# Three differences of two operands become one difference and four clamped tensor_scalar instructions in an RWKV and mixture-of-experts kernel

## The chip, the cores and the metric

The kernel runs on one core of a Trainium2 chip. Its time is the device time of one execution in microseconds (us), the median of three runs. A profile of one further execution gives every engine's instructions with their start and length. The engines are TensorE (PE, with its weight loads as PEld), VectorE (DVE), ScalarE (ACT), GpSimd (POOL) and SyncE (SP, which only issues DMAs here).

## What is computed

Sixteen sequences of 512 tokens and 256 channels go through two blocks, each with a layer norm ahead of it and a residual sum behind it. The first is an RWKV attention. Cut to what matters here:

```
w = -exp(time_decay)                 # per channel
step(aa, bb, pp; kk, vv):            # over the 512 tokens
    ww  = time_first + kk
    p   = max(pp, ww)
    y   = (exp(pp-p)*aa + exp(ww-p)*vv) / (exp(pp-p)*bb + exp(ww-p))
    p2  = max(pp + w, kk)
    e1  = exp(pp + w - p2);  e2 = exp(kk - p2)
    aa, bb, pp = e1*aa + e2*vv, e1*bb + e2, p2
out = (sigmoid(r) * y) @ Wo.T
```

The second block is a causal convolution and pointwise product, a router that picks two of eight experts for each token, the eight experts' products, a root-mean-square norm and a small feed-forward.

## The kernel before

The channels lie on the 128 partitions in two halves (H = 2), the tokens along the free axis, so a tile such as `fd` is 128 x 2 x 512 in f32. Every engine runs a program of its own, in an order written out by hand, and engines meet only at semaphores. One pass of `body(g, f, b, a, n)` works on five sequences at once, each in a later stage: n is normalised and turned, a goes through the recurrence, b through the output projection, f through router and experts, g through the norm and the feed-forward. `schedule` runs the body 20 times, for g = -4 to 15, of which g = 1 to 10 are a loop. A sequence is in stage a in 16 of these bodies: three while the pipeline fills (no g yet), and thirteen, g = 0 to 12, in which both a and g are there. The fill bodies g = -3 and g = -2 have an order of their own (the branch `if on(n) and not on(f)`).

The recurrence is made of scans along the tokens. `running_maximum` scans `pp` (L1128), one scan per half. `differences` writes `fd` = pp(t-1) - pp(t) (L1136) and `gd` = kk - pp(t) (L1137); `difference_sd`, which stands further back in the body, writes `sd` = kk - pp(t-1) (L1140). `decay` holds w. ACT turns `fd` into e1 with w as the bias of the exponential (L778), `gd` into e2 (L780), and `sd` into a sigmoid (L793). Each of the three differences raises the semaphore `diffs` by one. `wkv_step` 0 to 9 are the rest of the recurrence on DVE.

What matters of the order around this, in a body with a and g:

- DVE: scans of `pp`, `differences`, `mix` of xr (L1081), `scale_h(0)` (L1119, writes `hh`), `convolve` (L1073, four instructions), `scale_h(1)` (L1119 again), `difference_sd`, `quotient` (L1109), then `xh`, `wkv_step` 0 and 1, the sum `x1` (L1193), `x1l`, statistics, the copy of the router's logits `lg` (L1228), the picking of experts up to `gap` (L1261), and the weighted sums of the experts (L1295). `scale_h(1)` waits for `rms` from POOL (L413).
- PE: products of xk, xv and xr (L450), the turning of `hh` (L444), the pointwise product, `wdown` (L624), `wo` (L536), the router (L643 to L647), then sixteen groups of experts (L465 to L469) with other work between them.
- ACT: copies of `kk` and `vv`, the exponentials, squares for the norm (L749), tanh, copies of `ht`, the sigmoid, silu, `x1h` (L896), gelu, and then the sixteen silus of the experts (L729); the third of them stands behind `th` (L920), which needs `gap`.

The semaphore `diffs` is also read by the copy of `kk` and by `running_maximum` of the next sequence, which may overwrite `kk` and `pp` only when all differences are done.

Of the kernel before, what the change touches and what calls it, by code (L numbers as in the profile page):

```python
# [18 lines left out]
ALU = mybir.AluOpType  # L19
ACT = mybir.ActivationFunctionType  # L20
# [27 lines left out]
def build(nc, x, vecs, w_attn, w_pw, w_router, w_expert, w_out, w_down, w_up, b_rows, b_down, norm_w, out):  # L48
    B, T, C = x.shape
    H = C // P  # L50
# [9 lines left out]
    with ExitStack() as ctx:  # L60
        def sb(name, shape, dt=F32):
            return ctx.enter_context(nc.sbuf_tensor(name, shape, dt))
# [4 lines left out]
        def sig(name, per):  # L67
            return Signal(ctx.enter_context(nc.semaphore(name)), per)
# [3 lines left out]
        decay = sb("decay", [P, H])  # L72
# [17 lines left out]
        bias = sb("bias", [BP, NROW // BP])  # L90
# [30 lines left out]
        kk = sb("kk", [P, H, T])  # L121
        vv = sb("vv", [P, H, T])
        pp = sb("pp", [P, H, 1 + T])
        fd = sb("fd", [P, H, T])
        gd = sb("gd", [P, H, T])
        sd = sb("sd", [P, H, T])
# [80 lines left out]
        v_ready = sig("v_ready", 2)  # L207
        tr_ready = sig("tr_ready", 2)
        p_ready = sig("p_ready", 2)
        diffs = sig("diffs", 3)  # L210
        e1_ready = sig("e1_ready", 2)
        e2_ready = sig("e2_ready", 1)
        sg_ready = sig("sg_ready", 2)
# [54 lines left out]
        def on(seq):  # L268

            return not isinstance(seq, int) or 0 <= seq < B  # L270
# [413 lines left out]
        def _(act):  # L684
# [4 lines left out]
            def body(g, f, b, a, n):  # L689
# [83 lines left out]
                        act.copy(vv[:, h, :], pk[:, h, :]).then_inc(v_ready.sem, 1)  # L773

                def exponentials():
                    act.wait_ge(diffs.sem, diffs.at(a, 1))
                    for h in range(H):
                        act.activation(fd[:, h, :], fd[:, h, :], ACT.Exp, bias=decay[:, h:h + 1]).then_inc(e1_ready.sem, 1)  # L778
                    act.wait_ge(diffs.sem, diffs.at(a, 2))
                    act.activation(gd[:], gd[:], ACT.Exp).then_inc(e2_ready.sem, 1)  # L780

                def tanh_r():
# [5 lines left out]
                        act.activation(tr[:, h, :], pk[:, h, :], ACT.Tanh, scale=0.5).then_inc(tr_ready.sem, 1)  # L788

                def sigma():  # L790
                    act.wait_ge(diffs.sem, diffs.at(a, 3))
                    for h in range(H):
                        act.activation(sd[:, h, :], sd[:, h, :], ACT.Sigmoid, bias=neg_first[:, h:h + 1],  # L793
                                       scale=-1.0).then_inc(sg_ready.sem, 1)
# [69 lines left out]
                if on(a):  # L864
                    exponentials()
# [17 lines left out]
                if on(a):  # L883
                    sigma()
# [80 lines left out]
        def _(dve):  # L965
            v = nc.vector
# [41 lines left out]
            def body(g, f, b, a, n):  # L1008
# [39 lines left out]
                def residual(i):  # L1048

                    dve.wait_ge(xres_in.sem, xres_in.at(b))  # L1050
                    if on(f):
                        dve.wait_ge(xn2_ready.sem, xn2_ready.at(f))
                        dve.wait_ge(x2t_ready.sem, x2t_ready.at(f))
                    dve.wait_ge(wo_done.sem, wo_done.at(b, i + 1))
                    t = slice(2 * i, 2 * i + 2)
                    v.tensor_tensor(x2[:, t, :], po[:, i], xres[:, t, :], ALU.add).then_inc(x2_ready.sem, 1)

                def stats_proj():

                    dve.wait_ge(x2_ready.sem, x2_ready.at(b))  # L1060
                    if on(f):
                        dve.wait_ge(rstd2_ready.sem, rstd2_ready.at(f))
                    for t in range(NT):
                        v.bn_stats(st2[:, t, :], x2[:, t, :]).then_inc(stats2.sem, 1)

                def convolve(seq):

                    for tap in (1, 2):
                        for h in range(H):
                            dve.wait_ge(tap_ready.sem, tap_ready.at(seq, h + 1))  # L1070
                            if tap == 2:
                                dve.wait_ge(conv.sem, conv.at(seq, h + 1))
                            v.scalar_tensor_tensor(out=cv[:, h, :], in0=xt2[:, h, 2 - tap:2 - tap + T],  # L1073
                                                   scalar=vec[:, 7 - tap, h:h + 1], in1=cv[:, h, :],
                                                   op0=ALU.mult, op1=ALU.add).then_inc(conv.sem, 1)

                def mix(seq, m, dst):

                    for h in range(H):
                        dve.wait_ge(faded[m].sem, faded[m].at(seq, h + 1))  # L1080
                        v.scalar_tensor_tensor(out=dst[:, h, :], in0=xt1[:, h, 1:1 + T], scalar=vec[:, 2 + m, h:h + 1],  # L1081
                                               in1=dst[:, h, :], op0=ALU.mult, op1=ALU.add).then_inc(mixed.sem, 1)
# [12 lines left out]
                def stats_front():  # L1095

                    dve.wait_ge(x_in.sem, x_in.at(n))
                    if on(a):
                        dve.wait_ge(rstd1_ready.sem, rstd1_ready.at(a))
                    for t in range(NT):  # L1100
                        v.bn_stats(st1[:, t, :], xa[:, t, :]).then_inc(stats1.sem, 1)  # L1101

                def quotient():

                    dve.wait_ge(rec_ready.sem, rec_ready.at(b))
                    dve.wait_ge(wkv.sem, wkv.at(b))
                    if on(f):
                        dve.wait_ge(wo_done.sem, wo_done.at(f))
                    v.tensor_tensor(rwkv[:], num[:], den[:], ALU.mult).then_inc(rwkv_ready.sem, 1)  # L1109

                def scale_h(i):

                    dve.wait_ge(rms_ready.sem, rms_ready.at(g, 3 * i + 3))

                    if on(g - 1):
                        dve.wait_ge(t4_done.sem, t4_done.at(g - 1))
                        dve.wait_ge(xh_ready.sem, xh_ready.at(g - 1))
                    for t in range(2 * i, 2 * i + 2):
                        v.scalar_tensor_tensor(out=hh[:, t, :], in0=po[:, i, t % 2, :], scalar=rms[:, t:t + 1],  # L1119
                                               in1=normw[:], op0=ALU.mult, op1=ALU.mult).then_inc(h_ready.sem, 1)  # L1120

                def running_maximum():

                    if on(b):
                        dve.wait_ge(diffs.sem, diffs.at(b))
                    for h in range(H):
                        dve.wait_ge(k_ready.sem, k_ready.at(a, h + 1))
                        v.tensor_tensor_scan(pp[:, h, 1:1 + T], decay[:, h:h + 1].to_broadcast([P, T]), kk[:, h, :],  # L1128
                                             NEG_INF, ALU.add, ALU.max).then_inc(p_ready.sem, 1)

                def differences():
                    dve.wait_ge(p_ready.sem, p_ready.at(a))

                    if on(b):
                        dve.wait_ge(wkv.sem, wkv.at(b))
                    v.tensor_tensor(fd[:], pp[:, :, 0:T], pp[:, :, 1:1 + T], ALU.subtract).then_inc(diffs.sem, 1)  # L1136
                    v.tensor_tensor(gd[:], kk[:], pp[:, :, 1:1 + T], ALU.subtract).then_inc(diffs.sem, 1)  # L1137

                def difference_sd():
                    v.tensor_tensor(sd[:], kk[:], pp[:, :, 0:T], ALU.subtract).then_inc(diffs.sem, 1)  # L1140

                if on(n) and not on(f):

                    if on(b):
                        quotient()
                    if on(a):
                        mix(a, 2, xr)
                    stats_front()
                    if on(a):
                        running_maximum()  # L1150
                        differences()
                        difference_sd()
                    if on(b):
                        residual(0)
                        residual(1)
                        stats_proj()
                    if on(a):
                        for i in range(10):
                            wkv_step(i)
                    mix(n, 0, xk)  # L1160
                    if on(b):
                        convolve(b)
                    mix(n, 1, xv)
                    return

                if on(a):
                    running_maximum()
                    differences()
                    mix(a, 2, xr)
# [3 lines left out]
                    convolve(f)  # L1173
                if on(g):
                    scale_h(1)
                if on(a):
                    difference_sd()
                if on(b):
                    quotient()
                if on(g):  # L1180
# [129 lines left out]
                else:  # L1310
                    last_sum()

            schedule(dve, body, {-4: constants, -3: lambda: expert_high_part(0), -2: lambda: expert_high_part(1)})


# [34 lines left out]
```

## Time and profile before

| | |
|---|---|
| median of three runs | 982.94 us (982.54 to 983.36) |
| the profiled execution | 982.2 us |
| its span, first to last instruction | 980.4 us |
| mean granted TensorE clock | 0.965 |
| PE busy | 886.0 us, 90% |
| DVE busy | 863.2 us, 88% |
| ACT busy | 720.5 us, 73% |
| POOL busy | 227.5 us, 23% |

The 1.8 us between the profiled execution's time and its span lie outside the instructions. Busy shares are means over the span; in the thirteen full bodies, one every 55.5 us, PE and DVE are both busy nearly without a break.

### The profile page before, as it was taken

To read this page: it belongs to the slowest core of one execution; us is meant where nothing else is said; L and a number is where in the kernel's file an instruction comes from. 1 tells how busy PE (TensorE), PEld (TensorE's weight loads), DVE (VectorE), ACT (ScalarE), POOL (GpSimd) and SP (SyncE) were. 2 spreads that over 40 slices of the span, in tenths; PEclk is the share of its full clock that TensorE was granted. 3 is DMA by queue.
4 is the path that set the end of the run, shared out by engine and by line. 5 is a ranking of instruction groups with operands and counts; after the bars stand their busy time and mean duration, and the time that the engine had idled before them with its cause. 6 is when DMAs were issued, how large, how long until landed. Compare 5 with 4: busy or idle time off the path is not lost. (4 is left out here: it accounts for less than half of the span.)

```text
span 980.4 us, 15792 instructions
## 1 busy us (share of the span) xinstructions
PE 886.0 (90%) x4288; PEld 483.6 (49%) x4288; DVE 863.2 (88%) x1577; ACT 720.5 (73%) x1233; POOL 227.5 (23%) x477
## 2 busy tenths in 40 slices
PE   3554999999999999999999999999999999969895
PEld 2232455554555555554555555555555555535543
DVE  4999799999999999999999999999999998957562
ACT  4755688786978788787878788687878788545643
POOL 3485222113130222113130222113131221111000
PEclk9776999999999999999999999999999999979998
DMA  6110010101010010101010010101001000100000
GB/s 210 44 43 1 1 44 1 65 1 66 0 43 21 0 64 0 64 0 64 0 42 22 0 64 0 64 0 64 0 22 42 22 22 1 44 1 22 1 22 21
DMA packets 28772, 29.66 MB, mean 30 GB/s; under 512 B 2090, under 2 KB 28484, under 8 KB 28484
## 3 DMA queue, kind: packets, MB, share of 16 engines
q1 hardware_dynamic: 28740, 29.27, 8.8%
q8 instruction: 15, 0.25, 0.1%
q14 instruction: 17, 0.14, 0.0%
HBM read 20.87 MB, written 8.39 MB: 30 GB/s over the span
## 5 line engine op out<-in xcount | busy, mean ns | idle before, releaser
L1295 DVE SCALAR_TENSOR_TENSOR comb<-ye,rw,comb 128x256 f32<-128x256 f32 x448 | 216.3, 483 | 24.9 <-ACT ye L729 10.5
L729 ACT ACTIVATE ye<-pe 128x512 f32<-128x512 f32 x256 | 151.6, 597 | 105.2 <-PE pe L469 90.9
L469 PE MATMUL pe<-weh,x1l 128*128 128x512 f16 x512 | 194.0, 379 | 0.0
L468 PE MATMUL pe<-wel,x1h 128*128 128x512 f16 x512 | 194.0, 379 | 0.0
L467 PE MATMUL pe<-weh,x1h 128*128 128x512 f16 x512 | 194.0, 379 | 0.0
L409 POOL TENSOR_TENSOR msv<-ms,rms_eps_c 128x2 f32<-128x2 f32 x32 | 14.9, 466 | 398.0 <-ACT sq L749 398.0
L465 PE MATMUL pe<-brow,ones 128*128 128x512 f16 x256 | 97.3, 380 | 9.0 <-ACT ye L729 9.0
L380 POOL TENSOR_TENSOR mo<-st 128x4 f32<-128x4 f32 x32 | 12.1, 377 | 317.4 <-DVE st L1101 179.6
L468 PEld LDWEIGHTS pe<-wel,x1h 128*128 128x128 f16 x512 | 50.0, 98 | 60.5
L469 PEld LDWEIGHTS pe<-weh,x1l 128*128 128x128 f16 x512 | 50.1, 98 | 60.4
L467 PEld LDWEIGHTS pe<-weh,x1h 128*128 128x128 f16 x512 | 50.1, 98 | 50.3
L450 PE MATMUL pk<-xk,wa 128*128 128x512 f32 x128 | 64.4, 650 | 11.4 <-issue 8.5
L510 PE MATMUL po<-wout,combt 128*128 128x256 f32 x256 | 69.6, 394 | 0.0
L450 PE MATMUL pk<-xr,wa 128*128 128x512 f32 x128 | 60.3, 615 | 8.4 <-DVE xr L1081 8.4
L444 PE MATMUL pt<-ident,xn 128*128 128x128 f32 x256 | 37.4, 294 | 32.0 <-ACT xn L713 22.3
L450 PE MATMUL pk<-cv,wpw 128*128 128x512 f32 x128 | 59.9, 609 | 4.1 <-DVE cv L1073 4.1
L450 PE MATMUL pk<-xv,wa 128*128 128x512 f32 x128 | 58.7, 602 | 0.0
L536 PE MATMUL po<-wo,rwkv 128*128 128x256 f32 x256 | 58.4, 381 | 0.0
L536 PEld LDWEIGHTS po<-wo,rwkv 128*128 128x128 f32 x256 | 49.2, 192 | 14.1 <-issue 8.2
L444 PEld LDWEIGHTS pt<-ident,xn 128*128 128x128 f32 x256 | 31.3, 151 | 42.0 <-issue 26.4
L450 PEld LDWEIGHTS pk<-xk,wa 128*128 128x128 f32 x128 | 26.5, 210 | 41.5 <-issue 39.8
L1119 DVE SCALAR_TENSOR_TENSOR hh<-po,rms,normw 128x256 f32<-128x256 f32 x64 | 27.9, 478 | 21.3 <-POOL rms L413 21.3
(154 smaller groups left out, 1986.1 us busy)
## 6 DMA issues: line engine op xcount, KB each, us to landing
xa<-in_x SPq DMA_DIRECT2D x16, 512.0 KB, 3.6
xres<-in_x SPq DMA_DIRECT2D x16, 512.0 KB, 4.4
out_y<-yo SPq DMA_DIRECT2D x16, 512.0 KB, 2.9
ye<-in_w_expert SPq DMA_DIRECT2D x2, 1024.0 KB, 6.8
wa<-in_w_attn SPq DMA_DIRECT2D x1, 1024.0 KB, 7.8
wpw<-in_w_pw SPq DMA_DIRECT2D x1, 256.0 KB, 6.0
wout<-in_w_out SPq DMA_DIRECT2D x1, 256.0 KB, 6.2
wdown<-in_w_down SPq DMA_DIRECT2D x2, 64.0 KB, 4.7
```

The costliest lines, as they stand in the source:

```text
L409: nc.gpsimd.tensor_tensor(msv[:, t], ms[:, t], rms_eps_c[:, t], ALU.add).then_inc(rms_ready.sem, 1)
L444: mm = nc.tensor.transpose(pt[:, h, t * P:(t + 1) * P], src[:, t, h * P:(h + 1) * P], ident[:])
L450: mm = nc.tensor.matmul(dst, weight[:, h, m * P:(m + 1) * P], src[:, h, :], start=h == 0, stop=h == H - 1)
L465: nc.tensor.matmul(dst, ones2[:], brow[:, cols], start=True, stop=False)
L467: nc.tensor.matmul(dst, x1h[:, h, tok], weh[:, h, cols], start=False, stop=False)
L468: nc.tensor.matmul(dst, x1h[:, h, tok], wel[:, h, cols], start=False, stop=False)
L469: mm = nc.tensor.matmul(dst, x1l[:, h, tok], weh[:, h, cols], start=False, stop=h == H - 1)
L510: mm = nc.tensor.matmul(dst, combt[:, h, tok], wout[:, h, :], start=False, stop=h == H - 1)
L536: mm = nc.tensor.matmul(po[:, i, t % 2, :], rwkv[:, h, t * P:(t + 1) * P], wo2[:, h, :], start=h == 0, stop=h == H - 1)
L729: act.activation(ye[:, i % NY, :], pe[:, i % 2, :], ACT.Silu, scale=1.0 / WSCALE).then_inc(ye_ready.sem, 1)
L1119: v.scalar_tensor_tensor(out=hh[:, t, :], in0=po[:, i, t % 2, :], scalar=rms[:, t:t + 1], in1=normw[:], op0=ALU.mult, op1=ALU.mult).then_i ...
L1295: v.scalar_tensor_tensor(out=comb[:, t, :], in0=src, scalar=rw[:, t, e:e + 1], in1=comb[:, t, :], op0=ALU.mult, op1=ALU.add).then_inc(comb ...
```

## The change

`sd` is now the first difference, in place of `fd`. `fd` and `gd` are computed from it: pp(t) is the larger of pp(t-1) + w and kk, so that sd - w = kk - (pp(t-1) + w) is positive where kk is the larger. `fd` = max(sd - w, 0), of which ACT takes exp with a scale of -1 and without a bias, and `gd` = min(sd - w, 0). Each is a `tensor_scalar` with w as a per-partition scalar, one instruction per half, since w differs between the halves. DVE waits for `sd` on `diffs` before the first of them. `diffs` now rises by five a sequence. The exponentials wait for each half of `fd` apart, and the sigmoid waits for all five where it waited for all three. `difference_sd` is gone from its place behind `scale_h(1)`.

```diff
-        diffs = sig("diffs", 3)
+        diffs = sig("diffs", 5)
...
                 def exponentials():
-                    act.wait_ge(diffs.sem, diffs.at(a, 1))
-                    for h in range(H):
-                        act.activation(fd[:, h, :], fd[:, h, :], ACT.Exp, bias=decay[:, h:h + 1]).then_inc(e1_ready.sem, 1)
-                    act.wait_ge(diffs.sem, diffs.at(a, 2))
+                    for h in range(H):
+                        act.wait_ge(diffs.sem, diffs.at(a, 2 + h))
+                        act.activation(fd[:, h, :], fd[:, h, :], ACT.Exp, scale=-1.0).then_inc(e1_ready.sem, 1)
+                    act.wait_ge(diffs.sem, diffs.at(a, 5))
...
                 def sigma():
-                    act.wait_ge(diffs.sem, diffs.at(a, 3))
+                    act.wait_ge(diffs.sem, diffs.at(a))
...
-                    v.tensor_tensor(fd[:], pp[:, :, 0:T], pp[:, :, 1:1 + T], ALU.subtract).then_inc(diffs.sem, 1)
-                    v.tensor_tensor(gd[:], kk[:], pp[:, :, 1:1 + T], ALU.subtract).then_inc(diffs.sem, 1)
-
-                def difference_sd():
                     v.tensor_tensor(sd[:], kk[:], pp[:, :, 0:T], ALU.subtract).then_inc(diffs.sem, 1)
+                    dve.wait_ge(diffs.sem, diffs.at(a, 1))
+                    for h in range(H):
+                        v.tensor_scalar(fd[:, h, :], sd[:, h, :], decay[:, h:h + 1], 0.0, ALU.subtract,
+                                        ALU.max).then_inc(diffs.sem, 1)
+                    for h in range(H):
+                        v.tensor_scalar(gd[:, h, :], sd[:, h, :], decay[:, h:h + 1], 0.0, ALU.subtract,
+                                        ALU.min).then_inc(diffs.sem, 1)
...
                 if on(a):
-                    difference_sd()
-                if on(a):
                     quotient()
```

On DVE, in the bodies with a and g, the change reads so (rows with - as before, with + as now, a line number being that of its own kernel):

```order
 L1128 SCALAR_TENSOR_TENSOR pp<-decay,kk 128x512 x2
-L1136 TENSOR_TENSOR fd<-pp 128x1024
-L1137 TENSOR_TENSOR gd<-kk,pp 128x1024
+L1136 TENSOR_TENSOR sd<-kk,pp 128x1024
+L1139 TENSOR_SCALAR fd<-sd,decay 128x512 x2
+L1142 TENSOR_SCALAR gd<-sd,decay 128x512 x2
 L1081 SCALAR_TENSOR_TENSOR xr<-xt,vec,xr 128x512 x2
 L1119 SCALAR_TENSOR_TENSOR hh<-po,rms,normw 128x256 x2
 L1073 SCALAR_TENSOR_TENSOR cv<-xt,vec,cv 128x512 x4
 L1119 SCALAR_TENSOR_TENSOR hh<-po,rms,normw 128x256 x2
-L1140 TENSOR_TENSOR sd<-kk,pp 128x1024
 L1109 TENSOR_TENSOR rwkv<-num,den 128x1024
```

Ahead of xr and the two `hh` stood two instructions of 1024 elements; now one of 1024 and four of 512 stand there, and behind the second `hh` one of 1024 is gone.

On ACT, in the loop, the place of the exponentials (ISA and REGISTER_ALU rows are the sequencer's work for a wait in the loop):

```order
 L737 COPY combt<-pt 128x2x128
-L776 ISA
-L778 ACTIVATE fd<-fd,decay 128x512 x2
+L777 ISA
+L778 ACTIVATE fd<-fd 128x512
+L777 REGISTER_ALU
+L778 ACTIVATE fd<-fd 128x512
 L779 REGISTER_ALU
 L780 ACTIVATE gd<-gd 128x1024
```

The same three instructions stand there as before; the first two lose an operand and each gets a wait of its own.

## Rows read from the trace of the kernel before

**Rows 1.** The page, busy time and share of the span of each engine.

```profile
PE 886.0 (90%) x4288; PEld 483.6 (49%) x4288; DVE 863.2 (88%) x1577; ACT 720.5 (73%) x1233; POOL 227.5 (23%) x477
```

**Rows 2.** PE over time: start, length, instruction, count, idle time before it.

```profile
155.22 1.09 PE L444 MATMUL pt<-ident,hh 128*128 128x128 f32 x8 [0.76 <-DVE hh L1119]
...
372.34 3.63 PE L450 MATMUL pk<-xr,wa 128*128 128x512 f32 x8
376.79 1.09 PE L444 MATMUL pt<-ident,hh 128*128 128x128 f32 x8 [0.81 <-DVE hh L1119]
...
386.32 0.17 PE L643 MATMUL pk<-brow,ones 128*128 128x8 f16 x1
...
390.45 0.39 PE L465 MATMUL pe<-brow,ones 128*128 128x512 f16 x1 [0.24 <-ACT ye L729]
...
394.90 0.39 PE L465 MATMUL pe<-brow,ones 128*128 128x512 f16 x1 [0.36 <-ACT ye L729]
...
820.14 1.09 PE L444 MATMUL pt<-ident,hh 128*128 128x128 f32 x8 [0.81 <-DVE hh L1119]
```

**Rows 3.** DVE over time, the body of 366 to 421 us and the next scans.

```profile
366.06 2.34 DVE L1128 TENSOR_TENSOR_SCAN pp<-decay,kk 128x512 f32<-128x512 f32 x2 [0.26 <-ACT kk L765]
368.54 1.23 DVE L1136 TENSOR_TENSOR fd<-pp 128x1024 f32<-128x1024 f32 x1
369.68 1.22 DVE L1137 TENSOR_TENSOR gd<-kk,pp 128x1024 f32<-128x1024 f32 x1
370.81 1.41 DVE L1081 SCALAR_TENSOR_TENSOR xr<-xt,vec,xr 128x512 f32<-128x512 f32 x2
...
372.93 2.73 DVE L1073 SCALAR_TENSOR_TENSOR cv<-xt,vec,cv 128x512 f32<-128x512 f32 x4
375.86 0.88 DVE L1119 SCALAR_TENSOR_TENSOR hh<-po,rms,normw 128x256 f32<-128x256 f32 x2 [0.20 <-POOL rms L413]
376.65 1.22 DVE L1140 TENSOR_TENSOR sd<-kk,pp 128x1024 f32<-128x1024 f32 x1
...
387.31 0.19 DVE L1228 COPY lg<-pk 128x32 f32<-128x32 f32 x1 [0.73 <-PE pk L647]
...
389.84 0.16 DVE L1213 TENSOR_TENSOR hit<-lg,top 128x32 f32<-128x32 f32 x1
390.03 0.19 DVE L1215 TENSOR_TENSOR hit<-hit,rank 128x32 f32<-128x32 f32 x1
...
393.80 0.16 DVE L1261 TENSOR_TENSOR gap<-top 128x4 f32<-128x4 f32 x1
...
421.53 2.34 DVE L1128 TENSOR_TENSOR_SCAN pp<-decay,kk 128x512 f32<-128x512 f32 x2 [0.26 <-ACT kk L765]
```

**Rows 4.** ACT over time, the same body.

```profile
370.57 1.34 ACT L778 ACTIVATE fd<-fd,decay 128x512 f32<-128x512 f32 x2
371.81 1.05 ACT L780 ACTIVATE gd<-gd 128x1024 f32<-128x1024 f32 x1
...
394.08 0.20 ACT L920 ACTIVATE th<-gap 128x4 f32<-128x4 f32 x1 [3.15 <-DVE gap L1261]
```

**Rows 5.** Groups by line and shape, DVE: busy us, mean ns of one, idle time before.

```profile
L1291 DVE TENSOR_SCALAR comb<-ye,rw 128x256 f32<-128x256 f32 x64 | 22.3, 348 | 4.8 <-ACT ye L729 2.4 <-DVE rw L1277 2.2
...
L985 DVE TENSOR_SCALAR wo<-wa 128x512 f32<-128x512 f32 x1 | 0.4, 421 | 0.0
...
L997 DVE TENSOR_SCALAR wuh<-wup 128x256 f16<-128x256 f32 x1 | 0.3, 274 | 0.0
```

**Rows 6.** POOL over time, the same body.

```profile
374.46 1.09 POOL L411 TENSOR_TENSOR msp<-msv,minus_half 128x2 f32<-128x2 f32 x1
```

**Rows 7.** The fill: DVE over time in body g = -3.

```profile
28.79 1.23 DVE L1013 TENSOR_TENSOR ev<-gd,vv 128x1024 f32<-128x1024 f32 x1
...
46.70 1.23 DVE L1109 TENSOR_TENSOR rwkv<-num,den 128x1024 f32<-128x1024 f32 x1 [1.97 <-ACT den L757]
```

**Rows 8.** The fill: PE over time in body g = -1.

```profile
97.73 5.77 PE L450 MATMUL pk<-xr,wa 128*128 128x512 f32 x8 [8.38 <-DVE xr L1081]
```

More of the change, by code:

```diff
@@ L1175, in body @@
                     scale_h(1)
-                if on(a):
-                    difference_sd()
                 if on(b):
```

## The prediction

> **What bounds the kernel now.** The page comes first: PE is busy for 90% of the span and DVE for 88% [rows 1]. Two engines as full as that say nothing about which of them sets the time, so the second view is each engine over time through one body in the middle, 366.06 to 421.53 us, where the pipeline is full [rows 3]. The bodies repeat to some hundredths of a microsecond, and there are thirteen of them with a and g; the turning of `hh` on PE at 155.22 is the first and that at 820.14 the last [rows 2].
>
> The third view is what PE waits for in that body, since PE is the fullest. It stands still three times: 0.81 us before it turns `hh`, 0.24 us before the third group of experts, 0.36 us before the fifth [rows 2]. Follow each back.
>
> - `hh`: the product of xr ends at 372.34 + 3.63 = 375.97. DVE's second pair of `hh` starts at 375.86 and ends at 376.74, and PE turns it at 376.79 [rows 2, 3]. So DVE ends last there. On DVE all is back to back from the scans at 366.06, but for 0.20 us in which the pair waits for POOL's `rms` [rows 3].
> - The fifth group: its silu on ACT stands behind `th`, which waited 3.15 us for `gap` [rows 4]. `gap` is 6.5 us of unbroken DVE work behind `lg`, and `lg` waited 0.73 us for PE's router [rows 3]. The router runs at 386.32 as the end of a stretch in which PE doesn't stop after `hh` [rows 2].
> - From the fifth group on PE runs on into the next body; ACT's copy of `kk` releases DVE's next scans at 421.53, and 0.26 us of waiting ahead of them shows that DVE was ready for it [rows 3].
>
> That is a ring: scans, the two differences, xr, `hh`, `cv`, `hh` on DVE; `hh` to router on PE; `lg` to `gap` on DVE; `th` and a silu on ACT; groups of experts on PE; `kk`; scans again. What lengthens a link of it lengthens every body. `sd` at 376.65 stands in no link: it comes after the second `hh`, and DVE has those 0.73 us to spare before `lg` [rows 3]. The other idle stretch of PE, before the third group, goes back to `x1`, which does stand behind `sd`; but a shorter wait there only makes the one before the fifth group longer.
>
> **What the change moves.** It removes two differences of 1.22 us and adds four shorter instructions, but it also brings the one that stays from off the ring onto it.
>
> Durations overlap: `fd` runs 1.23 us, yet `gd` starts 1.14 after it, so a following instruction starts 0.08 to 0.09 us before the end of the one ahead. Where DVE waits for its own result this is lost: `hit` ends at 390.00 and its reader starts at 390.03 [rows 3].
>
> The trace has no tensor_scalar of 512 elements with a per-partition scalar and two operations. The nearest is one of 256 with such a scalar, 348 ns; 256 elements more cost 421 - 274 = 147 ns between the two with constants [rows 5]. That is some 0.48 to 0.50 us, and 0.40 from start to start, the value I take. From below: no surcharge for the scalar, 421 ns, 0.34 from start to start. From above: an instruction with two tensors and a scalar, as xr, whose pair takes 1.41 us, so 0.75 for one and 0.66 from start to start [rows 3].
>
> Now the ring. `sd` starts where `fd` did, 368.54, ends at 369.77, the first tensor_scalar starts at 369.80, and xr starts four steps of 0.40 later, at 371.40, in place of 370.81: 0.59 us late. Queued behind it are xr, `hh` and `cv`. PE's xr product starts at about 372.9 and ends at 376.5, which is still ahead of `hh`. `cv` ended at 375.66, so the second `hh` could have started at 375.58; POOL held it to 375.86, and 0.28 of the delay disappears in that wait. `hh` comes about **0.30 us later a body**. With the bounds of the tensor_scalar it is 0.07 (0.35 - 0.28) and 1.35 (1.63 - 0.28).
>
> The added wait of DVE for itself costs 0.12 us of the 0.59: 0.03 after the end in place of 0.09 before it [rows 3]. The Trainium skill, VectorE: DVE Perf Modes, section "The DRAIN you can't avoid", says that a semaphore after each of a chain of Vector instructions cost nothing over one at the end, and the section on rules for kernel authors that the count of instructions is what to keep low. By the first the delay would be 0.18 a body and the time 984.7 in place of 986.3; the rows here have the overlap, so I keep 0.30.
>
> What stays hidden. ACT takes the first exponential of `fd` when its copies are done, at 370.57, and the first half of `fd` is there at 369.80 + 0.48 = 370.28. `gd` is whole at 369.80 + 1.20 + 0.48 = 371.48, ahead of 371.81, at which its exponential began [rows 4]. So the squares, and POOL's `rms` behind them, are not late; and the exponentials of `fd`, which lose the bias, can only be shorter. With the dear tensor_scalar `gd` is whole at 372.54 and `rms` goes back by 0.7, still less than DVE's own 1.63. Behind the second `hh` DVE gains 1.14 - 0.30 = 0.84 us, up to `lg`. There it meets a router that is 0.30 late: the wait of 0.73 before `lg` becomes about 1.9, and nothing of the gain comes back. The sigmoid gets `sd` earlier, but on ACT it stands behind the copies of `ht`, which wait for PE.
>
> **The fill.** In g = -3 and -2 `sd` stood right behind `gd`, so the stretch is shorter by 3 x 1.14 - (1.23 + 0.03 + 1.60) = 0.56 us; but in g = -3 `ev` started when the exponential of `gd` released it [rows 7], and that now comes some 0.5 later. There DVE later waited 1.97 us for ACT [rows 7], whose chain begins with POOL's statistics, which run between DVE's instructions; shorter ones may let POOL through earlier, and at most about 1.5 us of that wait could go before DVE's own work, 0.5 later, is the limit. In g = -1 PE waited 8.38 us for xr [rows 8], which comes 0.59 later. Together between -2.1 (1.5 + 0.56) and +1.1 (0.5 + 0.59); I take the middle, -0.5. The drain has no stage a.
>
> **The sum.** 13 x 0.30 = 3.9, less 0.5, is +3.4 us: 982.2 of the profiled execution becomes 985.6. That execution lies 0.7 under the median of 982.94, so against the median it is 986.3.
>
> **The rivals.**
>
> *DVE's total sets the time.* Then what counts is the sum, not the place: -0.56 us in each of 16 sequences, 9 us, and 974. For it: DVE's 88%, and almost no idle time on it in a full body. Against it: its waits before the scans and `lg` grow with every cut behind `hh`. It decides if DVE, not PE, runs late at `lg`, that is if `lg` followed the statistics without a gap; it has 0.73 us [rows 3]. The Trainium skill, Perfetto Trace Analysis, section "Identifying the Most-Contended Engine", goes by occupancy for VectorE and would take the engine with the most first; by it less DVE work is a gain. 8%.
>
> *The slack takes it all.* The tensor_scalar costs its lower bound: 13 x 0.07 = 0.9, less 0.5, 983.3. For it: the 421 ns; against it: the scalar's price in the 348. 14%.
>
> *POOL's answer moves with DVE.* `msp` took 1.09 us while `cv` ran beside it [rows 6]. If the later `cv` instructions hold POOL back, `rms` comes as late as they do, the 0.28 is no slack, and each body pays 0.59: +7.2, 990.1. The Trainium skill, SBUF — State Buffer, section "SBUF: two separate sides", says that a GpSimd instruction and a Vector one with two SBUF inputs take a shared port pair exclusively, which would do this; no row says which instruction held `msp`. 12%.
>
> *The clamp runs at the upper bound.* 13 x 1.35 = 17.6, less 0.5: 1000.0. For it: two operations and a per-partition scalar in one instruction stand in no row; against it: L1291. 7%.
>
> **How the numbers follow.** My forecast has 59%, its own range 984.3 to 988.5 (0.20 to 0.45 a body and the fill's bounds in part). The range 981.8 to 991 takes in the second and third rival and leaves out the first and the fourth, 15%, and some tails. A change of 0.2%, 2.0 us, is about what can be told from none. Faster is the first rival, 8%. Same, 981.0 to 984.9, is the second and about a sixth of the forecast: 14 + 10 = 24%. The rest, 68%, is slower.
>
> **What would show it.** Right: four tensor_scalar of about 0.48 us, xr about 0.6 us later behind the scans, no wait for POOL before the second `hh`, bodies of 55.8 in place of 55.47 us, and a wait before `lg` near 1.9 us. Wrong: a body of 55.2 or less (the total counts), a POOL wait that is still there (the third rival), or a tensor_scalar near 0.75.

## The result, and the profile after

The changed kernel takes **1000.11 us** (median of 4 runs, 998.18 to 1000.86), the kernel before 983.15 in the same session: a ratio of **1.0178** (95% interval 1.0164 to 1.0192). It is slower by 17 us, where 3.4 were forecast.

The page of the changed kernel, its busy times:

```profile
PE 884.4 (89%) x4288; PEld 482.8 (48%) x4288; DVE 854.2 (86%) x1609; ACT 719.9 (72%) x1233; POOL 230.4 (23%) x477
```

Against [rows 1] DVE has 9.0 us less to do, as much as the first rival counted (16 x 0.56), and no engine has 17 us more. So the time went into waiting. DVE over time in the changed kernel, in the body that answers to [rows 3]:

```profile
370.83 2.34 DVE L1128 TENSOR_TENSOR_SCAN pp<-decay,kk 128x512 f32<-128x512 f32 x2 [0.26 <-ACT kk L765]
373.30 1.23 DVE L1136 TENSOR_TENSOR sd<-kk,pp 128x1024 f32<-128x1024 f32 x1
374.56 0.88 DVE L1139 TENSOR_SCALAR fd<-sd,decay 128x512 f32<-128x512 f32 x2
375.36 0.87 DVE L1142 TENSOR_SCALAR gd<-sd,decay 128x512 f32<-128x512 f32 x2
376.15 1.41 DVE L1081 SCALAR_TENSOR_TENSOR xr<-xt,vec,xr 128x512 f32<-128x512 f32 x2
377.48 0.87 DVE L1119 SCALAR_TENSOR_TENSOR hh<-po,rms,normw 128x256 f32<-128x256 f32 x2
378.26 2.73 DVE L1073 SCALAR_TENSOR_TENSOR cv<-xt,vec,cv 128x512 f32<-128x512 f32 x4
382.13 0.88 DVE L1119 SCALAR_TENSOR_TENSOR hh<-po,rms,normw 128x256 f32<-128x256 f32 x2 [1.14 <-POOL rms L413]
...
388.09 1.29 DVE L1193 TENSOR_TENSOR x<-x,xt 128x512 f32<-128x512 f32 x2 [0.42 <-ACT x L705]
...
393.58 0.19 DVE L1228 COPY lg<-pk 128x32 f32<-128x32 f32 x1 [1.33 <-PE pk L647]
...
400.00 0.16 DVE L1261 TENSOR_TENSOR gap<-top 128x4 f32<-128x4 f32 x1
...
427.73 2.34 DVE L1128 TENSOR_TENSOR_SCAN pp<-decay,kk 128x512 f32<-128x512 f32 x2 [0.26 <-ACT kk L765]
```

A body takes 427.73 - 370.83 = 56.90 us, before 55.47. Up to `cv` everything is where the prediction put it: the tensor_scalar groups, xr 5.32 us behind the scans in place of 4.75, and `cv` behind it. Then, where 0.20 us of waiting for POOL should have vanished, there are 1.14. POOL over time in the same stretch, first of the kernel before, then of the changed one:

```profile
374.00 0.39 POOL L409 TENSOR_TENSOR msv<-ms,rms_eps_c 128x2 f32<-128x2 f32 x1 [7.88 <-ACT sq L749]
...
375.63 0.20 POOL L413 TENSOR_TENSOR rms<-msp,sqrt_c 128x2 f32<-128x2 f32 x1
```

```profile
378.71 2.34 POOL L409 TENSOR_TENSOR msv<-ms,rms_eps_c 128x2 f32<-128x2 f32 x1 [7.83 <-ACT sq L749]
381.13 0.70 POOL L411 TENSOR_TENSOR msp<-msv,minus_half 128x2 f32<-128x2 f32 x1
381.90 0.20 POOL L413 TENSOR_TENSOR rms<-msp,sqrt_c 128x2 f32<-128x2 f32 x1
```

POOL's first step, `msv`, adds a constant to two numbers of each partition. It comes 7.88 us behind the scans in the changed kernel and 7.93 in that before, so it isn't late. But it takes 2.34 us in place of 0.39, and its end at 381.05 lies 0.05 behind the end of the last `cv` (378.26 + 2.73 = 380.99). Two more steps must follow before `rms` is there. The four `cv` instructions, one behind the other, are called the row below. POOL is let in where a step of it gets through as one `cv` hands over to the next, and shut out where it has to wait for the end of the row. That the lost time is `msv`'s is seen in the groups by line, POOL of before and then of the changed kernel (busy us, mean ns):

```profile
L409 POOL TENSOR_TENSOR msv<-ms,rms_eps_c 128x2 f32<-128x2 f32 x32 | 14.9, 466 | 398.0 <-ACT sq L749 398.0
```

```profile
L409 POOL TENSOR_TENSOR msv<-ms,rms_eps_c 128x2 f32<-128x2 f32 x32 | 40.2, 1256 | 396.0 <-ACT sq L749 388.4 <-DVE hh L1119 7.5
```

What PE makes of it, PE over time in the changed kernel, to be held against [rows 2]:

```profile
377.61 3.70 PE L450 MATMUL pk<-xr,wa 128*128 128x512 f32 x8 [0.34 <-DVE xr L1081]
383.06 1.09 PE L444 MATMUL pt<-ident,hh 128*128 128x128 f32 x8 [1.75 <-DVE hh L1119]
...
401.10 0.39 PE L465 MATMUL pe<-brow,ones 128*128 128x512 f16 x1 [0.70 <-ACT ye L729]
```

The sum by stretches, from scan to scan. The first full body's scans start at 143.53 and the last one's at 825.80 us, before at 144.59 and 809.52:

```profile
143.53 2.34 DVE L1128 TENSOR_TENSOR_SCAN pp<-decay,kk 128x512 f32<-128x512 f32 x2 [0.75 <-ACT kk L765]
...
825.80 2.33 DVE L1128 TENSOR_TENSOR_SCAN pp<-decay,kk 128x512 f32<-128x512 f32 x2
```

The fill gained 1.06, the twelve bodies between lost 682.27 - 664.93 = 17.34, the rest gained 0.29: +15.99 of span (the profiled execution of the changed kernel, 998.18 us, is the fastest of its four). So the thirteenth body's delay isn't found at the end, though its second `hh` comes 1.5 us late too.

### The profile page after: what moved, and what is told of

Same layout as the page of the kernel before. It is cut to its first block and busy times, and to the rows that moved or that the text cites. A ratio compares the mean times of both kernels' runs of the same rounds, so it can differ in the third digit from the quotient of the medians.

```text
span 996.4 us, 15834 instructions
## 1 busy us (share of the span) xinstructions
PE 884.4 (89%) x4288; PEld 482.8 (48%) x4288; DVE 854.2 (86%) x1609; ACT 719.9 (72%) x1233; POOL 230.4 (23%) x477
## 5 line engine op out<-in xcount | busy, mean ns | idle before, releaser
L409 POOL TENSOR_TENSOR msv<-ms,rms_eps_c 128x2 f32<-128x2 f32 x32 | 40.2, 1256 | 396.0 <-ACT sq L749 388.4
L393 POOL TENSOR_TENSOR pw<-mo,minus_half 128x4 f32<-128x4 f32 x32 | 54.2, 1695 | 2.5
```

Of the source, the lines that this page charges most:

```text
L393: nc.gpsimd.tensor_tensor(pw[:, 0], mo[:, 3], minus_half[:], ALU.pow).then_inc(ready.sem, 1)
L409: nc.gpsimd.tensor_tensor(msv[:, t], ms[:, t], rms_eps_c[:, t], ALU.add).then_inc(rms_ready.sem, 1)
```

## The experiments

The theories. **A**: `msv` is shut out by the row of `cv` until the row ends, because the row comes later; the ring pays for it. **B**: a row that is merely later costs its lateness, and the hold comes from the tensor_scalar themselves. **C**: ACT's shorter exponentials shift what follows. Later ones: **D**, one tensor_scalar ahead is enough to shut POOL out; **E**, two in a row; **F**, the place of DVE's last rest ahead of the row; **G**, the four half-size instructions. `msv`, the start of the second `hh` behind the scans, and the body are those of full bodies; before has 0.39, 9.80 and 55.47, the changed kernel 2.34, 11.30 and 56.90 us.

**e1: the kernel before, with `cv` later.**

```diff
                     differences()
+                    v.memset(idle[:], 0.0)
                     mix(a, 2, xr)
```

> The kernel before, with one VectorE memset of 512 elements, which nobody reads, between the two differences and xr in the bodies that have the router in flight; it delays xr, hh and cv by about 0.6 us a body, as the change does, with none of the change's arithmetic. If POOL's first small addition is held by the row of cv instructions, and the hold depends on where it falls in that row (theory A), POOL waits as in the changed kernel: msv 1 to 2.4 us in place of 0.39, a body of 56.4 to 56.9 us and 995 to 1001 us. If the tensor_scalar instructions themselves hold POOL or VectorE (theory B), nothing of that is here: msv 0.4 us, a body of about 55.8 and 986 to 988 us.

985.38 us, 1.0036 (1.0021 to 1.005); body 55.77, `msv` 0.19. `cv` was 0.42 us later, in the changed kernel 0.57, and POOL still got in. In e8 and e13, below, it gets in at 0.53 and at 0.70. Lateness alone doesn't do it: the first half of A falls.

**e2: the changed kernel, the exponentials of `fd` with a bias again (a column of zeros).**

```diff
-                        act.activation(fd[:, h, :], fd[:, h, :], ACT.Exp, scale=-1.0).then_inc(e1_ready.sem, 1)
+                        act.activation(fd[:, h, :], fd[:, h, :], ACT.Exp, bias=xt1[:, h, 0:1], scale=-1.0).then_inc(e1_ready.sem, 1)
```

> The changed kernel, its exponentials of fd with a bias operand of zeros, so that each costs ScalarE what it cost before; the squares and POOL's msv then come 0.2 us later against VectorE. If the shorter exponentials brought POOL to a bad moment (theory C), the time falls to 984 to 988 us. By theory A the hold starts 0.2 us later in the same row of cv: it can end at any of the row's boundaries, so between 985 and 1000 us, and hh follows rms by 0.03 us whichever it is. By theory B nothing changes: 1000 us.

999.77, 1.0181 (1.0159 to 1.0202); body 56.90, `msv` 2.29, though it comes 7.93 behind the scans, as before. C falls.

**e3 and e4: the row of `cv` cut in two by the first `hh` pair, in the changed kernel and in that before.**

```diff
-                def convolve(seq):
+                def convolve(seq, taps=(1, 2)):
...
+                early_cv = on(f) and on(a) and not is_first(f)
+                if early_cv:
+                    convolve(f, (1,))
                 if on(g):
                     scale_h(0)
-                if on(f) and on(a) and not is_first(f):
-                    convolve(f)
+                if early_cv:
+                    convolve(f, (2,))
                 if on(g):
                     scale_h(1)
```

> The changed kernel with the first two cv instructions ahead of the first hh pair and the last two behind it, in place of four in a row. The hh pair reads PSUM and one SBUF tile, so by theory A POOL gets through beside it: msv about 0.25 us, rms ready ahead of the end of cv, no wait for POOL before the second hh, a body of 55.75 us, 984 to 988 us. By theory B and C it stays near 1000 us.

> The kernel before with the same new place of the first hh pair. By theory A POOL's rms comes earlier than VectorE needs it and the 0.20 us of waiting before the second hh goes: 0.2 to 0.28 us a body, 979 to 981 us. By theory B and C there is no hold of POOL by cv to remove: 983 us.

e3: 986.52, 1.004 (1.0028 to 1.0052), body 55.85. e4: 982.19, 0.9996 (0.9984 to 1.0007), body 55.46. POOL over time in e3:

```profile
375.39 0.23 POOL L409 TENSOR_TENSOR msv<-ms,rms_eps_c 128x2 f32<-128x2 f32 x1 [7.82 <-ACT sq L749]
375.69 0.69 POOL L411 TENSOR_TENSOR msp<-msv,minus_half 128x2 f32<-128x2 f32 x1
376.47 1.26 POOL L413 TENSOR_TENSOR rms<-msp,sqrt_c 128x2 f32<-128x2 f32 x1
```

`msv` is let in where the second `cv` hands over to the first `hh`, `msp` runs beside that `hh`, unheld, and only `rms` waits for the last two `cv`. The ring has 13.6 of the 17 us back. With the row out of `msv`'s way the change costs 986.52 - 982.19 = 4.3 us, near the 3.4 forecast. In the kernel before, the cut gained nothing (a miss): the hold moved on to `msp`, 1.28 us.

**e5 and e8: the kernel before, with one unread tensor_scalar of 512, or two of 256, in the place of e1's memset.**

```diff
                     differences()
+                    v.tensor_scalar(idle[:], kk[:, 0, :], decay[:, 0:1], 0.0, ALU.subtract, ALU.max)
                     mix(a, 2, xr)
```

> The kernel before with one tensor_scalar of 512 elements (per-partition scalar, two operations, result unread) where the first experiment had a memset of the same length. It delays xr, hh and cv as the memset did. In the six profiles so far POOL's msv got in between two cv instructions wherever no tensor_scalar stood ahead in VectorE's unbroken row, and never where one did. If that is the cause (theory D: from a tensor_scalar on, until VectorE comes to rest, POOL gets in at no seam between two instructions with two SBUF inputs), msv takes 2.2 to 2.4 us, a body 56.8 us, and the run 998 to 1001 us. If not (the place or the number of instructions matters), it is as with the memset: msv 0.2 us, 55.8 us, 985 to 987 us.

> The kernel before with two tensor_scalar instructions of 256 elements back to back (results unread) where the fifth run had one of 512. One alone did not shut POOL out of the row of cv. If two in a row do, as four do in the changed kernel (theory E), msv takes 2.2 to 2.4 us, a body 56.8 us, 998 to 1001 us. If not, msv 0.2 to 0.8 us, 55.8 us, 984 to 987 us.

e5: 984.63, 1.0035 (1.0021 to 1.0049), body 55.85, `msv` 0.79. e8: 988.2, 1.0064 (1.0046 to 1.0081), body 55.85, `msv` 0.25. The times miss the ranges of their branches, by 0.4 us below (e5) and 1.2 above (e8), but POOL got in in every full body: D and E fall.

**e9: the changed kernel, each tensor_scalar as a scalar_tensor_tensor with a column of zeros.**

```diff
-                        v.tensor_scalar(fd[:, h, :], sd[:, h, :], decay[:, h:h + 1], 0.0, ALU.subtract,
-                                        ALU.max).then_inc(diffs.sem, 1)
...
+                        v.scalar_tensor_tensor(out=fd[:, h, :], in0=sd[:, h, :], scalar=decay[:, h:h + 1],
+                                               in1=xt1[:, h, 0:1].to_broadcast([P, T]), op0=ALU.subtract,
+                                               op1=ALU.max).then_inc(diffs.sem, 1)
...
```

> The changed kernel with its four tensor_scalar written as scalar_tensor_tensor with a zero column as third operand: same values, same places, no tensor_scalar, 0.74 us each in place of 0.48. VectorE is then 1.06 us later at cv than in the changed kernel, and hh comes 1.35 us later than before by VectorE alone. If the tensor_scalar instructions are what shuts POOL out, msv gets in at the first seam (under 0.8 us) and VectorE doesn't wait for POOL; the time is then about the same by another road, 998 to 1003 us. If the missing rest alone is the cause, whatever the instructions, msv is held to the end of cv again and hh comes 2.3 to 2.6 us late: 1010 to 1014 us.

1017.06, 1.0353 (1.0335 to 1.037); body 57.97. The second `hh` comes 2.57 us later than before, as the second branch has it; the time lies 3 us above that branch's range. No tensor_scalar stands ahead of `cv`, and POOL is shut out all the same, POOL over time:

```profile
386.29 2.59 POOL L409 TENSOR_TENSOR msv<-ms,rms_eps_c 128x2 f32<-128x2 f32 x1 [8.64 <-DVE hh L1119]
```

B falls: it doesn't take a tensor_scalar.

**e6, e13 and e12: a rest of DVE ahead of the row.** e6 waits for the last `gd` before xr, e13 between the two pairs; each is a gap of about 35 ns. e12 puts that rest into the kernel before, where the changed one has it.

```diff
                     differences()
+                    dve.wait_ge(diffs.sem, diffs.at(a))
                     mix(a, 2, xr)
```

> The changed kernel with one more wait of VectorE for its own result: xr waits until all five instructions of the differences are done, which brings VectorE to rest for some 0.03 us and costs 0.12 us a body. By theory D msv then gets in at the first seam of cv (0.2 to 0.6 us), rms comes at the end of cv, a body takes 55.85 to 56.0 us and the run 986 to 990 us. If the hold has to do with the late cv alone, nothing changes but for 0.12 a body: 1000 to 1002 us.

> The changed kernel with one wait more on VectorE between the two tensor_scalar of fd and the two of gd, on the second fd: a 35 ns rest in the middle of the four, 0.12 us of start time for what stands behind. If a rest helps wherever it breaks the row of four: msv below 0.6 us, the second hh pair about 10.4 us behind the scan, body 55.9 to 56.1, 987 to 991 us, as with the rest behind all four. If only a rest behind the last of them helps: msv 2.2 to 2.4, the second hh pair at 11.4, body 57.0, 1000 to 1003 us.

> The kernel before with one wait more on VectorE between the differences fd and gd, on fd itself, which ends long before anything needs it: VectorE rests about 35 ns at the place (3.70 us behind the scan) where the changed kernel rests before its first tensor_scalar, and with no half-size instruction in the row. Theory F (it is the place of the last rest, so far ahead of the row of cv, that shuts POOL out): msv is held to the end of the row, about 1.8 to 2.4 us in place of 0.39, the second hh pair starts 10.8 to 10.9 us behind the scan in place of 9.80, body 56.4 to 56.6, 995 to 999 us. Theory G (it takes the four half-size instructions): msv 0.39 to 0.6, the second hh pair at 9.9 to 10.0, body 55.5 to 55.65, 983 to 985 us.

e6: 989.42, 1.0075 (1.0058 to 1.0092), body 55.97, `hh` 10.38. e13: 988.46, 1.0064 (1.0047 to 1.0081), 55.98, 10.38. e12: 982.46, 1.0003 (0.9993 to 1.0012), 55.59, 9.92. One wait more, which nothing needs, saves the changed kernel 11 us. It also moves the row by 0.12 us, and no run does that without a rest; so it isn't shown that the rest as such lets POOL in. POOL over time in e13:

```profile
376.00 0.47 POOL L409 TENSOR_TENSOR msv<-ms,rms_eps_c 128x2 f32<-128x2 f32 x1 [7.83 <-DVE hh L1119]
376.55 1.09 POOL L411 TENSOR_TENSOR msp<-msv,minus_half 128x2 f32<-128x2 f32 x1
377.71 0.75 POOL L413 TENSOR_TENSOR rms<-msp,sqrt_c 128x2 f32<-128x2 f32 x1
```

`msv` is let in where the first `cv` hands over to the second. In e12 the place of the rest alone did no harm, `msv` 0.51: F falls, and the time lies just below G's branch.

**e14: `fd` and `gd` by one tensor_scalar of 1024 each, with the first half's w for both halves.**

```diff
-                    for h in range(H):
-                        v.tensor_scalar(fd[:, h, :], sd[:, h, :], decay[:, h:h + 1], 0.0, ALU.subtract,
-                                        ALU.max).then_inc(diffs.sem, 1)
...
+                    v.tensor_scalar(fd[:], sd[:], decay[:, 0:1], 0.0, ALU.subtract, ALU.max).then_inc(diffs.sem, 1)
+                    v.tensor_scalar(gd[:], sd[:], decay[:, 0:1], 0.0, ALU.subtract, ALU.min).then_inc(diffs.sem, 1)
```

> The changed kernel with fd and gd made by one tensor_scalar of 1024 each in place of two of 512, with the first head's exponent for both heads (so the second head's weights are other numbers): about 0.88 us each, xr at the same 5.3 us behind the scan, two instructions fewer and no half-size one between sd and xr. If the number or the half size of the four matters: msv below 0.6 us, body 55.7 to 56.0, 985 to 989 us. If neither does: msv 2.3, the second hh pair at 11.3, body 56.9, 998 to 1001 us.

988.51 (985.62 to 990.09), 1.0073 (1.0053 to 1.0092). The instruction takes 0.75 us, not 0.88, so xr comes 0.26 earlier than in the changed kernel. The time is that of the first branch, and `msv` is that of neither. The finding is another: in one execution POOL got in in eleven full bodies and was shut out in two. POOL in the body of 366.50 and in the next, of 422.20:

```profile
374.38 0.75 POOL L409 TENSOR_TENSOR msv<-ms,rms_eps_c 128x2 f32<-128x2 f32 x1 [7.81 <-ACT sq L749]
375.21 1.09 POOL L411 TENSOR_TENSOR msp<-msv,minus_half 128x2 f32<-128x2 f32 x1
376.37 0.20 POOL L413 TENSOR_TENSOR rms<-msp,sqrt_c 128x2 f32<-128x2 f32 x1
...
430.08 2.08 POOL L409 TENSOR_TENSOR msv<-ms,rms_eps_c 128x2 f32<-128x2 f32 x1 [7.82 <-ACT sq L749]
432.23 0.69 POOL L411 TENSOR_TENSOR msp<-msv,minus_half 128x2 f32<-128x2 f32 x1
433.01 0.20 POOL L413 TENSOR_TENSOR rms<-msp,sqrt_c 128x2 f32<-128x2 f32 x1
```

and DVE in the same two:

```profile
373.67 2.73 DVE L1073 SCALAR_TENSOR_TENSOR cv<-xt,vec,cv 128x512 f32<-128x512 f32 x4
376.60 0.88 DVE L1119 SCALAR_TENSOR_TENSOR hh<-po,rms,normw 128x256 f32<-128x256 f32 x2 [0.20 <-POOL rms L413]
...
429.37 2.73 DVE L1073 SCALAR_TENSOR_TENSOR cv<-xt,vec,cv 128x512 f32<-128x512 f32 x4
433.24 0.88 DVE L1119 SCALAR_TENSOR_TENSOR hh<-po,rms,normw 128x256 f32<-128x256 f32 x2 [1.13 <-POOL rms L413]
```

Both rows of `cv` start 7.17 us behind their scans and both `msv` arrive 7.88 behind them; the bodies take 55.70 and 56.64 us. The same program, with everything where it was to 0.01 us, paid 0.94 us in the second of them and not in the first. So no count of instructions and no arrival that the trace can show decides it alone; and POOL is shut out without the four half-size instructions, so that G isn't needed.

**e15: the changed kernel, POOL's chain one multiplication shorter.**

```diff
-                nc.gpsimd.tensor_tensor(msp[:, t], msv[:, t], minus_half[:, t], ALU.pow).then_inc(rms_ready.sem, 1)
-                pool.wait_ge(rms_ready.sem, rms_ready.at(seq, 3 * i + 2))
-                nc.gpsimd.tensor_tensor(rms[:, t], msp[:, t], sqrt_c[:, t], ALU.mult).then_inc(rms_ready.sem, 1)
...
+                nc.gpsimd.tensor_tensor(rms[:, t], msv[:, t], minus_half[:, t], ALU.pow).then_inc(rms_ready.sem, 1)
...
+                v.tensor_scalar(normw[:], normw[:], float(C) ** 0.5, None, ALU.mult).then_inc(dve_const.sem, 1)
```

> The changed kernel with POOL's chain one multiplication shorter (the power goes straight into rms, the norm's weights are scaled by 16 once at the start). Theory A (the loss is msv held to the end of the row of cv, and what POOL has left to do behind it is on the ring): one step of 0.20 with its start of 0.08 goes, the second hh pair at 11.03 us behind the scan in place of 11.30, body 56.6, 995 to 998 us. If POOL's chain was not on the ring: no change, 998 to 1001 us.

996.7, 1.0148 (1.0124 to 1.0171); `msv` 2.36, `hh` at 11.03, body 56.63. The second half of A holds: what POOL does behind the hold lies on the ring, the second `hh` to a hundredth. DVE over time in one body of e15:

```profile
370.94 2.34 DVE L1127 TENSOR_TENSOR_SCAN pp<-decay,kk 128x512 f32<-128x512 f32 x2 [0.25 <-ACT kk L763]
...
381.97 0.88 DVE L1118 SCALAR_TENSOR_TENSOR hh<-po,rms,normw 128x256 f32<-128x256 f32 x2 [0.86 <-POOL rms L411]
...
427.57 2.34 DVE L1127 TENSOR_TENSOR_SCAN pp<-decay,kk 128x512 f32<-128x512 f32 x2 [0.25 <-ACT kk L763]
```

**e7, e10 and e11: the same edit on the kernel before (e7); then the picks from `lg` to `gap` put in one stretch behind `lg`, ahead of the steps of the recurrence (e10); and both with e6's rest on the changed kernel (e11).**

```diff
                     largest(0, lg)
-                if on(a):
-                    wkv_step(3)
-                if on(f):
                     ranked(0, lg)
...
```

> The kernel before with POOL's chain for the norm one multiplication shorter (normw is scaled by 16 once at the start, and rms is the power itself). rms then comes 0.28 us earlier and the 0.20 us of waiting before the second hh goes: if the ring through hh sets the time, 0.2 to 0.28 us a body, 979 to 981 us; if VectorE's total does, 983 us.

> The kernel before with the shorter POOL chain, and the picking of experts up to gap right behind lg, ahead of the scans and sums that stood between its steps. If the ring (hh, router, lg, gap, th, groups) sets the time, gap comes some 4.5 us earlier, PE's wait before the fifth group goes and a body falls from 55.18 to 54.4 to 54.9 us: 968 to 975 us. If VectorE's total is already what counts, the steps' extra waits for themselves make it 978 to 985 us.

> The same with the change and the rest behind its four tensor_scalar. VectorE has 0.45 us less to do a body and its hh comes 0.7 us later than in the tenth run. If the link through hh still counts, it is slower than the tenth run by 0.3 to 0.7 us a body, 974 to 984 us; if with gap out of the way VectorE's total counts, it is faster than the tenth, by up to 0.45 a body, 963 to 972 us.

e7: **977.6, 0.9954 (0.9937 to 0.997)**: the fastest of all, body 55.17, no wait before the second `hh`:

```profile
364.29 2.34 DVE L1127 TENSOR_TENSOR_SCAN pp<-decay,kk 128x512 f32<-128x512 f32 x2 [0.26 <-ACT kk L763]
...
373.80 0.88 DVE L1118 SCALAR_TENSOR_TENSOR hh<-po,rms,normw 128x256 f32<-128x256 f32 x2
...
419.45 2.34 DVE L1127 TENSOR_TENSOR_SCAN pp<-decay,kk 128x512 f32<-128x512 f32 x2 [0.26 <-ACT kk L763]
```

e10: 981.26, 0.9995 (0.9985 to 1.0006), body 55.49: a miss. `gap` comes 1.79 us behind `lg`, but DVE now reaches the scans without a wait, in that body:

```profile
386.05 0.19 DVE L1227 COPY lg<-pk 128x32 f32<-128x32 f32 x1 [0.73 <-PE pk L645]
387.84 0.16 DVE L1240 TENSOR_TENSOR gap<-top 128x4 f32<-128x4 f32 x1
...
420.57 2.34 DVE L1127 TENSOR_TENSOR_SCAN pp<-decay,kk 128x512 f32<-128x512 f32 x2
```

From `lg` to the next scans, 34.52 us, DVE's own work is the longest way there. e11: 992.53, 1.0107 (1.0086 to 1.0128), body 56.20: a miss too, above both of its ranges. Against e10 its body is longer by 0.71 and its second `hh` later by 0.69, so the link through `hh` still counts.

## Why the prediction was wrong

**The ring was right.** e1, e7 and e15 move the second `hh` by +0.30, -0.28 and -0.27 us and the body by +0.30, -0.29 and -0.27. What the second `hh` loses, the body loses. Only the number of bodies was off: 13 were counted, and in the changed kernel twelve pay.

**The clamp was right.** 0.48 us each, 0.40 from start to start, xr 0.57 later against 0.59. The added wait costs what was said: `fd` starts 0.036 us behind the end of `sd`, where the next one starts 0.08 ahead of an end. The 1000.0 that the fourth rival gave is met by coincidence; its tensor_scalar near 0.75 did not occur.

**The step that failed** is the one that let 0.28 us of the delay disappear in the wait for POOL: "So the squares, and POOL's `rms` behind them, are not late". The squares are not late, as the arrival of `msv` shows. But the 0.28 was taken off as if `rms` had a time of its own, and that time hangs on the row: in the kernel before `msv` ended with the second `cv`, in the changed kernel with the fourth. The sign was in the trace of before, where `msv` took 0.39 us; unheld it takes 0.19 (e1). The prediction didn't read that line. So the term of -0.28 was +0.94: `hh` loses 0.57 (the row is later) + 0.94 (the wait for POOL grows from 0.20 to 1.14) = 1.51; 0.07 come back between `lg` and `gap`, 6.42 against 6.49 us, and 1.43 a body is left, where 0.30 was forecast. Twelve such bodies are the 17.34 us between the first scans and the last.

**The third rival named the mechanism** and gave it too small a price, 0.59 a body, and 12%. It let POOL's answer come as late as `cv`, with the same 0.20 behind it. The mechanism has a dearer end: if `cv` holds the first of the three steps to its own end, 0.05 + 0.08 + 0.70 + 0.08 + 0.20 + 0.03 = 1.14 us follow (the tail of `msv`, a start, `msp` unheld, a start, `rms`, the start of `hh`). With the 0.57, and less the 0.20 of before, that is the 1.51 us, and neither the forecast nor the rival had it.

The Trainium skill, SBUF — State Buffer, section "SBUF: two separate sides", says that whichever of a DVE instruction with two SBUF inputs and a GpSimd instruction that reads SBUF starts first gets the shared port pair for the whole instruction and the other blocks. The rows agree as far as the ends go: a held `msv` ends 0.05 to 0.06 us behind the end of a `cv`, in every full body of every run with the row of four. Of a row of overlapping instructions it doesn't say who is next, and e14 shows both outcomes at one arrival.

**Behind the second `hh`** the wait before `lg` was to be 1.9 us; it is 1.33, and another 0.42 went into a wait for ACT's `x`. On ACT that stands behind the copies of `ht`, which wait 1.81 us for PE's turning of `hh`, before 0.87. **The fill** gained 1.06 against 0.5, within its bounds; DVE's wait of 1.97 us there [rows 7] is gone, and POOL's chain of statistics ends at 29.35 us, before at 34.68: it did get through earlier there.

**What stays open.** That the hold is `msv` against the row of `cv`, and what it costs, is shown: by e3, which takes the row out of its way, by e15, and by e14, body against body. What decides the handovers isn't. The changed kernel loses all three in every full body, as do e2, e9 and e15; the kernel before, e1, e5 to e8 and e10 to e13 win at least one. Lateness, ACT, one or two tensor_scalar, the instruction's kind and the place of the rest were each tried, and none explains it alone. Nor does the place in the row at which `msv` arrives: in the changed kernel that is 0.45 us behind the start of `cv` in the body shown above and 0.06 in the last full one, and it is shut out in both; in e13 it is 0.32 and 0.01, and it is let in. The last full bodies, DVE and POOL over time, first of the changed kernel, then of e13:

```profile
833.13 2.73 DVE L1073 SCALAR_TENSOR_TENSOR cv<-xt,vec,cv 128x512 f32<-128x512 f32 x4
...
833.19 2.73 POOL L409 TENSOR_TENSOR msv<-ms,rms_eps_c 128x2 f32<-128x2 f32 x1 [7.25 <-ACT sq L749]
```

```profile
823.18 2.73 DVE L1073 SCALAR_TENSOR_TENSOR cv<-xt,vec,cv 128x512 f32<-128x512 f32 x4
...
823.19 0.78 POOL L409 TENSOR_TENSOR msv<-ms,rms_eps_c 128x2 f32<-128x2 f32 x1 [7.33 <-ACT sq L749]
```

e14 suggests a matter of timing finer than the trace resolves, which a repeated program may meet the same way in every body; that is argued, not shown.

## What to carry to other kernels

A wait for an engine that works between the instructions of another is no slack: when the row is moved, price the answer both as let in and as shut out to the end of the row, with every step that follows. Look at such short steps whose length varies (0.39, 0.19, 2.34 us for the same two numbers); they show who is holding them. Shortening the chain behind them paid in both kernels (e7 and e15). Cutting the row (e3) or one more wait ahead of it (e6, e13) paid in the changed kernel alone; in the kernel before they gained nothing (e4, e12).

## What the runs showed of the hardware

- A POOL step of 0.19 us took up to 2.78 us beside a row of four overlapping DVE instructions (e9). With a rest of DVE of 35 ns 3 us earlier, which also moved the row by 0.12 us, it took 0.47 in place of 2.34 (e13).
- With the row, the arrival and the instructions the same, POOL was let in in one body and not in the next (e14).
- A tensor_scalar with a per-partition scalar takes 0.48 us for 512 elements and 0.75 for 1024, 0.40 and 0.67 from start to start.
